# Sorting the edges of a graph layer: turned keys and weights copied bank by bank, the last seven swaps moved behind the sort, the first 128 columns ahead of the rest

## The chip, the cores and the metric

The kernel runs on one core of one Trainium2 chip. The metric is the device time of one execution in microseconds (us). Three runs of the kernel before gave 2411.13, 2404.05 and 2411.05 us, with the median 2411.05. A further execution was profiled: it took 2398.86 us, and its trace spans 2397.1 us. Engines are named as the profile names them: PE (matmuls), PEld (its weight loads), DVE (vector), ACT (scalar), POOL (GpSimd) and SP (which issues transfers).

## What is computed

The reference is a layer on a graph with 6250 nodes, 256 features and 100,000 edges, followed by a mixture of 16 experts. Only its first part matters here:

```python
feats = jnp.einsum('nf,hfo->hno', xn, W)                  # 4 heads of 64
z = s_self[:, edge_row] + s_neigh[:, edge_col]
e = jnp.where(z > 0, z, 0.2 * z) * edge_weight
alpha = segment_softmax(e, edge_row)                      # per row of the graph
out = segment_sum(alpha[:, None] * feats[edge_col], edge_row)
x = x + relu(out + bias) + mix(xn)                        # mix: linear attention
x = x + ffn(layernorm(x))                                 # top 2 of 16 experts
```

The edges come in no order of `src` that the kernel may rely on. It sorts them by `src` itself, with the destination in the low bits of each key and the edge's weight carried along. It can then sum the edges of a node tile with matmuls.

## The kernel before

**Stage one** is `nodes_and_sort`. It normalises 49 tiles of 128 nodes, projects them (PE, with POOL and ACT beside it) and stores the features to HBM (`feat_d`) for the gathers of stage two. In the same block DVE runs a bitonic sort of 128 x 784 (padded to 896) keys. Keys and weights lie in `big`, each in two buffers of 128 x 896 (`key`, `wgt`), and the steps go from one buffer to the other.

- A **swap** compares columns at a distance of 2^bit. DVE writes the mask, the minima and the maxima (L507 to L509; L511 to L513 where the columns don't pair evenly). ACT copies the old weights into the other buffer (L296), and DVE then exchanges the weights whose mask is set with a predicated copy (L522; L527 and L528). A predicated copy waits for the mask and for ACT's copy; ACT's next copy waits for the predicated copy.
- A **turn** transposes the 128 x 896 array, since swaps reach over columns only. PE transposes seven blocks of 128 columns into two PSUM banks of 512 columns, first the keys (into `p_turn`, then a semaphore `k_turned`), then the weights (into `p_kv`, then `w_turned`). DVE copies the keys back (L448, with a piece of 16 x 128 at L450 for turns back). ACT copies the weights back (L306, L308), and after that does its copy for the next swap (L296). There are 20 turns.
- A **sign** step flips the sign of some keys in place (L478).

A planner with costs (3.0 for a swap, 4.0 for a turn) puts 108 of the 190 steps beside the node tiles, where PE is busy. The other 82 are `rest`, run alone, with nine turns among them. The last of `rest` are a turn and the seven swaps of bits 6 to 0. Then the stage ends, and all engines meet at a barrier.

**Stage two** is `edge_stream`. The sorted edges are 784 used chunks of 128 edges each (one partition of one block of 128 columns is a chunk). Wherever a chunk crosses into another node tile it is taken once for each, which gives 832 places of (chunk, tile) pairs, in 26 blocks of 32. A preparation on DVE, PE and ACT builds for each pair its chunk number, its destinations (`pair_idx`), weights (`pair_w`) and places in the tile: masks of 128 x 416 (L1208), a matmul that counts them, one-hot picks (L1225), matmuls that select columns (L1154), and copies out of PSUM on ACT (L985, L989). In the trace the PSUM tiles are all named `wide`.

Then, for each pair, POOL issues an indirect DMA that gathers 128 rows of `feat_d` into a ring of 64 places in `big` (L934). It begins when ACT has copied the first half of `pair_idx` (`pool.wait_ge(pair_copied, 1)`). From the 65th on it waits until PE has summed the pair that held the place 64 before. DVE needs the 32 gathers of block k before it makes the scores of block k (L1301); it does this ten pairs into the summing of block k-1. From the scores come, over DVE, PE and ACT, the softmax numerators. Then for each pair ACT scales the rows (L961), PE sums them (L1057), and DVE adds the sum to the node tile (L1367). The first 13 blocks also carry the key-value products of the linear attention.

After stage two come routing, experts and the output. They read nothing else from the sort.

Of the kernel before, what the change touches and what calls it, by code (L numbers as in the profile page):

```python
# [61 lines left out]
def nodes_and_sort(nc, ctx, a, m):  # L62
# [31 lines left out]
    def inside(lo, *dims):  # L94
# [55 lines left out]
        sem("k_turned"), sem("w_turned"), sem("k_back"), sem("w_back"), sem("signed"))  # L150
    half_signed, masked, part_made, parity_made = sem("half_signed"), sem("masked"), sem("part_made"), sem("parity_made")
# [21 lines left out]
    m["sorted_in"] = buf  # L173

# [38 lines left out]
    with nc.Block() as block:  # L213
# [72 lines left out]

        def copy_weights(act, entry):

            kind, k, arg, buf, late, without, n = entry
            if kind == "swap":  # L290
                cols = slice(0, live(k, arg >= 7))
                if n["swap"]:
                    act.wait_ge(w_swapped, n["swap"])
                if n["turn"]:
                    act.wait_ge(w_back, n["turn"])
                nc.scalar.activation(wgt[:, 1 - buf, cols], wgt[:, buf, cols], ACT.Copy).then_inc(w_copied, 1)  # L296

        def weights_back(act, entry, via):
# [4 lines left out]
            to = wgt[:, 1 - buf, :]  # L303
            act.wait_ge(w_turned, n["turn"] + 1)
            width = live(k, True) if arg else WHOLE
            ins = nc.scalar.activation(to[:, 0:width], via[:, 0:width], ACT.Copy)  # L306
            if not arg and not without:
                ins = nc.scalar.activation(to[0:LATE, WHOLE:WIDE], via[0:LATE, WHOLE:WIDE], ACT.Copy)  # L308
            ins.then_inc(w_back, 1)

        @block.scalar
        def _(act):
# [57 lines left out]
            for entry in rest:  # L370
                copy_weights(act, entry)
                weights_back(act, entry, p_kv[1])

        @block.vector
        def _(dve):
# [67 lines left out]
            def keys_back(entry):  # L443
                kind, k, turned, buf, late, without, n = entry
                to = key[:, 1 - buf, :]
                dve.wait_ge(k_turned, n["turn"] + 1)
                width = live(k, True) if turned else WHOLE
                ins = nc.vector.tensor_copy(to[:, 0:width], p_turn[:, 0:width])  # L448
# [38 lines left out]
            def swap(entry):  # L487
# [32 lines left out]
                dve.wait_ge(masked, n["swap"] + 1)  # L520
                if whole:
# [34 lines left out]
        def _(pe):  # L556
# [24 lines left out]
            def keys_over(entry):  # L581
# [66 lines left out]
def edge_stream(nc, ctx, a, m):  # L648
# [116 lines left out]
    last = big[0:1, 4 * CH:4 * CH + PAIRS]  # L765
# [1591 lines left out]
```

## Time and profile before

| what | before |
|---|---|
| runs, median (lowest to highest) | 2411.05 us (2404.05 to 2411.13) |
| profiled execution, its span | 2398.86 us, 2397.1 us |
| node tiles end, sort runs alone from about | 333 us |
| last swap of the sort ends | 531 us |
| first gather starts | 546.37 us |
| last gather starts | 1613.89 us |
| stage two ends about | 1667 us |
| experts and output | 1800 to 2397 us |

Over the whole span PE is busy 70% of the time, DVE 73%, ACT 58% and POOL 55%. These are means over very different stages, and the table says where each begins. A row of the timeline gives start, duration, engine, line, operation, out<-in with shapes, and in brackets how long the engine had been idle before and what released it.

### The profile page before, as it was taken

To read this page: it belongs to the slowest core of one execution; us is meant where nothing else is said; L and a number is where in the kernel's file an instruction comes from. 1 tells how busy PE (TensorE), PEld (TensorE's weight loads), DVE (VectorE), ACT (ScalarE), POOL (GpSimd) and SP (SyncE) were. 2 spreads that over 40 slices of the span, in tenths; PEclk is the share of its full clock that TensorE was granted. 3 is DMA by queue.
4 is the path that set the end of the run, shared out by engine and by line. 5 is a ranking of instruction groups with operands and counts; after the bars stand their busy time and mean duration, and the time that the engine had idled before them with its cause. 6 is when DMAs were issued, how large, how long until landed. Compare 5 with 4: busy or idle time off the path is not lost. (4 is left out here: it accounts for less than half of the span.)

```text
span 2397.1 us, 38652 instructions
## 1 busy us (share of the span) xinstructions
PE 1681.5 (70%) x8046; PEld 1259.4 (53%) x8046; DVE 1756.0 (73%) x4645; ACT 1393.3 (58%) x4627; POOL 1309.4 (55%) x1245
## 2 busy tenths in 40 slices
PE   3899961115676777777767888766641999999965
PEld 2455531012454555555445555533541999999854
DVE  6988899985588888899867777677860555555468
ACT  2555553322687887879786878796430444444344
POOL 2333310006777777777777777770575555555521
PEclk9999985557678777767888989888555999999988
DMA  6333320005456565564746555541970333333354
GB/s 206 132 124 138 135 88 0 0 29 173 141 153 203 165 201 165 165 196 138 221 136 180 151 159 154 163 115 37 259 102 18 104 106 106 103 105 106 95 176 153
DMA packets 167253, 317.72 MB, mean 133 GB/s; under 512 B 34358, under 2 KB 102627, under 8 KB 167089
## 3 DMA queue, kind: packets, MB, share of 16 engines
q1 hardware_dynamic: 104654, 166.68, 20.9%
q0 software_dynamic: 54176, 140.57, 20.7%
q10 hardware_dynamic: 8256, 8.68, 2.0%
q8 instruction: 55, 0.90, 0.2%
q14 instruction: 112, 0.89, 0.1%
HBM read 248.17 MB, written 67.65 MB: 132 GB/s over the span
## 5 line engine op out<-in xcount | busy, mean ns | idle before, releaser
L934 POOL DMA_INDIRECT big<-feat_d,pair_idx x832 | 815.3, 980 | 265.7 <-issue 188.9
L961 ACT ACTIVATE big<-big 128x64 f32<-128x64 f32 x3328 | 800.5, 333 | 0.9
L1057 PE MATMUL wide<-big 128*128 128x260 f32 x1664 | 606.5, 488 | 152.8 <-DVE big L1367 113.7
L1057 PEld LDWEIGHTS wide<-big 128*128 128x128 f32 x1664 | 332.8, 231 | 249.9 <-issue 210.6
L1367 DVE TENSOR_TENSOR big<-big,wide 128x260 f32 x832 | 350.9, 422 | 119.1 <-PE wide L1057 52.5
L1348 DVE TENSOR_TENSOR big<-wide,pair_rel 128x128 f32<-128x128 f32 x832 | 233.6, 282 | 0.0
L296 ACT ACTIVATE big<-big 128x896 f32<-128x896 f32 (+2 forms) x153 | 136.9, 895 | 161.4 <-DVE big L522 147.6
L2051 PEld LDWEIGHTS p_h<-xT,w_sb 128*128 128x128 f32 x1808 | 220.4, 193 | 5.7
L2051 PE MATMUL p_h<-xT,w_sb 128*128 128x128 f32 x1808 | 220.8, 276 | 0.0
L268 POOL TENSOR_SCALAR xn<-X,mean,rstd 128x256 f32<-128x256 f32 x49 | 101.8, 2078 | 210.4 <-PE p_t L600 177.8
L2062 PE MATMUL p_o<-w_sb,hT 128*128 128x256 f32 x904 | 213.9, 379 | 1.1 <-DVE w_sb L2000 1.1
L2000 DVE COPY w_sb<-big 128x1024 f32 x113 | 84.1, 744 | 169.9 <-PE p_o L2062 169.9
L1941 POOL DMA_INDIRECT moe_d<-x_out,x_to x113 | 115.5, 1022 | 151.1 <-DVE x_idx L1980 111.2
L1955 ACT ACTIVATE xT<-p_x 128x256 f32<-128x256 f32 x113 | 43.4, 384 | 256.1 <-PE p_x L2040 256.1
L522 DVE COPY_PREDICATED big<-big 128x896 f32<-128x896 uint32 (+2 forms) x150 | 163.9, 1093 | 23.2 <-ACT big L296 22.8
L625 PE MATMUL p_kv<-big,xnT_s 128*128 128x512 f32 x392 | 177.2, 595 | 0.0
L2062 PEld LDWEIGHTS p_o<-w_sb,hT 128*128 128x128 f32 x904 | 162.9, 190 | 19.0 <-DVE w_sb L2000 1.5
L1964 ACT ACTIVATE hT<-p_h,b1T 128x128 f32<-128x128 f32 x452 | 128.9, 368 | 58.5 <-issue 54.4
L1933 POOL DMA_INDIRECT xs<-y_d,x_idx x113 | 130.4, 1154 | 46.3 <-issue 34.2
L1024 PEld LDWEIGHTS wide<-score_parts,hot_t 128*128 128x128 bf16 x832 | 91.0, 109 | 99.1 <-issue 47.6
L1633 POOL DMA_INDIRECT list_d<-pair_i,place_i x98 | 103.0, 1052 | 53.5 <-issue 29.6
L573 PE MATMUL p_turn<-ident,big 128*128 128x128 f32 x120 | 22.3, 337 | 156.0 <-DVE big L509 152.7
(329 smaller groups left out, 2675.9 us busy)
## 6 DMA issues: line engine op xcount, KB each, us to landing
big<-code_d SPq DMA_DIRECT2D x52, 512.0 KB
kv_d<-big SPq DMA_DIRECT2D x49, 512.0 KB, 2.6
X<-kv_d SPq DMA_DIRECT2D x12, 2048.0 KB, 13.0
big<-in_L_ffn_w_dram SPq DMA_DIRECT2D x32, 512.0 KB
b_sb<-in_L_ffn_b_dram SPq DMA_DIRECT2D x113, 128.0 KB, 3.0
big<-feat_d,pair_idx POOLq DMA_INDIRECT x832
big<-moe_d SPq DMA_DIRECT2D x7, 1792.0 KB, 9.9
feat_d<-feat_sb SPq DMA_DIRECT2D x49, 130.0 KB, 2.7
```

The lines of the kernel that those rows point to most:

```text
L296: nc.scalar.activation(wgt[:, 1 - buf, cols], wgt[:, buf, cols], ACT.Copy).then_inc(w_copied, 1)
L522: ins = nc.vector.copy_predicated(paired(w2[:, 0:whole], bit), mk.bitcast(U32).unsqueeze(2).to_broadcast([P, whole >> (bit + 1), 2, 1 << b ...
L625: last = nc.tensor.matmul(p_kv[par][:, n * INNER:(n + 1) * INNER], xnT_s[:, par, b, :], wqkv[:, b, (n + 1) * INNER:(n + 2) * INNER], start ...
L934: nc.gpsimd.indirect_dma_start(out=rows[:, n // SB % RB, n % SB, :], out_offset=None, in_=m["feat_d"], in_offset=bass.IndirectOffsetOnAxis ...
L961: ins = nc.scalar.activation(rows[:, b, s, cols], rows[:, b, s, cols], ACT.Copy, scale=rows[:, b, s, HF + h:HF + h + 1])
L1057: nc.tensor.matmul(sums[s % RING][:, 0:HF + H], onehot[:, s // GP % 2, s % GP, :], rows[:, b, s, :], start=True, stop=True).then_inc(summe ...
L1348: nc.vector.tensor_tensor(onehot[:, at // GP, at % GP, :], lane_p, pair_rel[:, ds(k * SB + s, 1)].to_broadcast([P, P]), ALU.is_equal).then ...
L1367: nc.vector.tensor_tensor(of, of, sums[s % RING][:, 0:HF + H], ALU.add).then_inc(added, 1)
L1933: nc.gpsimd.indirect_dma_start(out=xs[:, w, :], out_offset=None, in_=m["y_d"], in_offset=bass.IndirectOffsetOnAxis(idx[:, w:w + 1].bitcast ...
L1964: last = nc.scalar.activation(hT[:, par, f, :], p_h[par][:, f * P:(f + 1) * P], ACT.Relu, bias=b1T[:, ds(e * FB + f, 1)])
L2051: last = nc.tensor.matmul(p_h[par][:, cols], w1[:, par, b * F + f * P:b * F + (f + 1) * P], xT[:, par, b, :], start=(b == 0), stop=(b == K ...
L2062: last = nc.tensor.matmul(p_o[par][:, 0:D], hT[:, par, f, :], w2[:, at:at + D], start=(f == 0), stop=(f == FB - 1))
```

## The change

Three things are edited.

1. **Turns.** PE signals after the first four transposes (the first bank) as well as after all seven. DVE copies the keys of the first bank, 128 x 512, and then the other 256 or 272 columns. ACT copies the weights in the same two pieces.
2. **Weights behind the nodes.** For the turns of `rest` but the first, the weights aren't copied back into `wgt` first. The first swap after such a turn takes them from the PSUM bank: ACT makes its one copy from `p_kv`, and DVE's predicated copy reads `p_kv`.
3. **The last seven swaps** leave `nodes_and_sort`, which now ends with the turn. `edge_stream` begins with them, split in two. First all seven for the keys of columns 0 to 127, then from their first 128 chunks the first 64 entries of `pair_idx`, with the seven weight swaps of these columns around it. Then follow the seven swaps of the other 768 columns. POOL waits for the first 64 entries alone (`f_copied`) and for the old semaphore only at the 65th gather.

```diff
+    plan, final = plan[:-7], plan[-7:]
+    m["final"] = [(j, at) for _, _, j, at, *_ in final]
...
+    looped = plan[at][-1]["turn"]
+    straight = {n["swap"]: arg >= 7 for kind, k, arg, buf, late, without, n in rest
+                if kind == "swap" and n["turn"] > looped and arg in (6, k - 1)}
...
+        def turned_weights(act, to, via, turns, width, tail, done):
+            width = WHOLE if tail else width
+            act.wait_ge(w_first, turns)
+            nc.scalar.activation(to[:, 0:512], via[:, 0:512], ACT.Copy)
+            act.wait_ge(w_turned, turns)
+            ins = nc.scalar.activation(to[:, 512:width], via[:, 512:width], ACT.Copy)
+            if tail:
+                ins = nc.scalar.activation(to[0:LATE, WHOLE:WIDE], via[0:LATE, WHOLE:WIDE], ACT.Copy)
+            ins.then_inc(done, 1)
...
             if kind == "swap":
-                cols = slice(0, live(k, arg >= 7))
+                width = live(k, arg >= 7)
+                if n["swap"] in straight:
+                    turned_weights(act, wgt[:, 1 - buf, :], p_kv[1], n["turn"], min(width, LIVE), width == WIDE, w_copied)
+                    return
...
             for entry in rest:
                 copy_weights(act, entry)
-                weights_back(act, entry, p_kv[1])
+            assert rest[-1][0] == "turn"
+            weights_back(act, rest[-1], p_kv[1])
...
+                width = live(k, True) if turned else WHOLE
+                dve.wait_ge(k_first, n["turn"] + 1)
+                nc.vector.tensor_copy(to[:, 0:512], p_turn[:, 0:512])
                 dve.wait_ge(k_turned, n["turn"] + 1)
-                ins = nc.vector.tensor_copy(to[:, 0:width], p_turn[:, 0:width])
+                ins = nc.vector.tensor_copy(to[:, 512:width], p_turn[:, 512:width])
...
+                if n["swap"] in straight:
+                    w1 = p_kv[1]
...
-                flip(entry, key, p_turn, 0, range(7)).then_inc(k_turned, 1)
+                flip(entry, key, p_turn, 0, range(4)).then_inc(k_first, 1)
+                flip(entry, key, p_turn, 0, range(4, 7)).then_inc(k_turned, 1)
...
-                    pe.wait_ge(w_back, n["turn"])
-                flip(entry, wgt, via, 0, range(7)).then_inc(w_turned, 1)
+                    pe.wait_ge(w_back, min(n["turn"], looped))
+                flip(entry, wgt, via, 0, range(4)).then_inc(w_first, 1)
+                flip(entry, wgt, via, 0, range(4, 7)).then_inc(w_turned, 1)
...
-            pool.wait_ge(pair_copied, 1)
+            pool.wait_ge(f_copied, 1)
             for n in range(PAIRS):
+                if n == F:
+                    pool.wait_ge(pair_copied, 1)
...
+            for n in range(4):
+                copy_lead(n)
+            act.wait_ge(f_idx, 1)
+            nc.scalar.activation(pair_idx[:, 0:F], first_idx, ACT.Copy).then_inc(f_copied, 1)
+            for n in range(4, 7):
+                copy_lead(n)
+            for n, (_, at) in enumerate(m["final"]):
+                if n:
+                    act.wait_ge(rest_weights, n)
+                nc.scalar.activation(m["wgt"][:, 1 - at, P:CH], m["wgt"][:, at, P:CH], ACT.Copy).then_inc(rest_copied, 1)
...
+            pe.wait_ge(f_passes, 1)
+            nc.tensor.matmul(first_chunk, ones_b, first_passes, start=True, stop=True).then_inc(f_chunk, 1)
+            pe.wait_ge(f_code, 1)
+            pe.wait_ge(f_pick, 1)
+            nc.tensor.matmul(first_idx, first_dst, first_pick, start=True, stop=True).then_inc(f_idx, 1)
...
+            def swap_keys(bit, at, cols, mk, masked, swapped):
+                lo, hi = halves(m["key"][:, at, cols], bit)
+                to = halves(m["key"][:, 1 - at, cols], bit)
+                nc.vector.tensor_tensor(folded(mk, bit), lo, hi, ALU.is_gt).then_inc(masked, 1)
+                nc.vector.tensor_tensor(to[0], lo, hi, ALU.min)
+                nc.vector.tensor_tensor(to[1], lo, hi, ALU.max).then_inc(swapped, 1)
...
+            for n, (bit, at) in enumerate(m["final"]):
+                if n:
+                    dve.wait_ge(lead_keys, n)
+                swap_keys(bit, at, LEAD, lead_mask(n), lead_masked, lead_keys)
+            dve.wait_ge(lead_keys, 7)
             nc.vector.memset(first_row[:, HF:HF + H], TINY).then_inc(first_made, 1)
             dve.wait_ge(first_in, 16)
...
+            nc.vector.tensor_scalar(first_passes, iota_f[:, 0:F], step_f[:, 0:1], None, ALU.is_gt).then_inc(f_passes, 1)
...
+            nc.vector.tensor_scalar(first_dst, first_code[:, 0:P], N - 1, None, ALU.min).then_inc(f_code, 1)
+            for n in range(3):
+                lead_swap(n)
+            dve.wait_ge(f_chunk, 1)
+            nc.vector.tensor_scalar(first_pick, first_chunk, place_f[:, 0:1], None, ALU.is_equal).then_inc(f_pick, 1)
+            for n in range(3, 7):
+                lead_swap(n)
+            for n in range(7):
+                rest_swap(n)
```

`lead_swap(n)` is the predicated copy of step n over columns 0 to 127 (it waits for ACT's copy n and for the lead swap before it), and `rest_swap(n)` is a whole swap over the other 768.

The order in which the instructions stand shows the move. DVE at the end of the sort, before (`X` holds the bias row there, `ahead` begins the preparation):

```order
L507 TENSOR_TENSOR big<-big 128x448
L508 TENSOR_TENSOR big<-big 128x448
L509 TENSOR_TENSOR big<-big 128x448
L522 COPY_PREDICATED big<-big 128x896
L213 UNCONDITIONAL_BRANCH
L1189 UNCONDITIONAL_BRANCH
L1195 MEMSET X 128x4
L1197 TENSOR_SCALAR X<-X 128x256
L1199 TENSOR_SCALAR ahead<-place_f 128x7
```

The same place now, where the two branches are the barrier:

```order
L466 COPY big<-p_turn 128x256
L468 COPY big<-p_turn 16x128
L220 UNCONDITIONAL_BRANCH
L1246 UNCONDITIONAL_BRANCH
L1262 TENSOR_TENSOR big<-big 128x64
L1263 TENSOR_TENSOR big<-big 128x64
L1264 TENSOR_TENSOR big<-big 128x64
```

and, after the seven lead swaps of the keys, the first pairs' chain and the rest:

```order
L1313 TENSOR_SCALAR big<-big,step_f 128x64
L1314 TENSOR_SCALAR big<-big 128x128
L1315 TENSOR_SCALAR big<-big 128x128
L1269 COPY_PREDICATED big<-big 128x128 x3
L1319 TENSOR_SCALAR big<-wide,place_f 128x64
L1269 COPY_PREDICATED big<-big 128x128 x4
L1262 TENSOR_TENSOR big<-big 128x384
L1263 TENSOR_TENSOR big<-big 128x6x64
L1264 TENSOR_TENSOR big<-big 128x6x64
L1269 COPY_PREDICATED big<-big 128x768
```

So the barrier has moved ahead of the seven swaps, and `ahead` and all that follows it stand behind them. ACT at the last two turns, before:

```order
L306 ACTIVATE big<-p_kv 128x784
L296 ACTIVATE big<-big 128x784 x10
L306 ACTIVATE big<-p_kv 128x768
L308 ACTIVATE big<-p_kv 16x128
L296 ACTIVATE big<-big 128x896 x7
L213 UNCONDITIONAL_BRANCH
L938 UNCONDITIONAL_BRANCH
L985 ACTIVATE hot_t<-wide 128x416
```

and now:

```order
L298 ACTIVATE big<-p_kv 128x512
L300 ACTIVATE big<-p_kv 128x272
L317 ACTIVATE big<-big 128x784 x9
L298 ACTIVATE big<-p_kv 128x512
L300 ACTIVATE big<-p_kv 128x256
L302 ACTIVATE big<-p_kv 16x128
L220 UNCONDITIONAL_BRANCH
L972 UNCONDITIONAL_BRANCH
L1022 ACTIVATE big<-big 128x128 x4
L1027 ACTIVATE pair_idx<-wide 128x64
L1022 ACTIVATE big<-big 128x128 x3
L1033 ACTIVATE big<-big 128x768 x7
```

The ten copies of `wgt` after a turn have become nine, since the first one now comes from PSUM, and the small copy of `pair_idx` stands ahead of the seven copies of the rest. On POOL only the wait in front of the 832 gathers differs.

## Rows read from the trace of the kernel before

**Rows 1.** Page, costliest groups: count, busy us, mean ns, idle before, releaser.

```profile
L934 POOL DMA_INDIRECT big<-feat_d,pair_idx x832 | 815.3, 980 | 265.7 <-issue 188.9
```

**Rows 2.** Timeline of POOL: the first, the 32nd and the last of 832 gathers.

```profile
546.37 1.52 POOL L934 DMA_INDIRECT big<-feat_d,pair_idx  x1 [12.59 <-ACT pair_idx L989]
...
588.15 0.94 POOL L934 DMA_INDIRECT big<-feat_d,pair_idx  x1 [0.30 <-issue]
...
1613.89 0.95 POOL L934 DMA_INDIRECT big<-feat_d,pair_idx  x1 [0.30 <-issue]
```

**Rows 3.** Gathers in one stretch: length, busy us (count), PEclk, DMA share, GB/s.

```profile
717.00:1173.00 456.00, 348.79 (x353) 0.75 0.57 175
```

**Rows 4.** Timeline of DVE, line L1301: the scores of single blocks.

```profile
590.96 0.37 DVE L1301 TENSOR_TENSOR z<-wide,big 128x128 f32<-128x128 f32 x1 [13.07 <-DMA big<-feat_d,pair_idx]
631.54 0.38 DVE L1301 TENSOR_TENSOR z<-wide,big 128x128 f32<-128x128 f32 x1 [11.92 <-DMA big<-feat_d,pair_idx]
674.15 0.38 DVE L1301 TENSOR_TENSOR z<-wide,big 128x128 f32<-128x128 f32 x1 [1.79 <-DMA big<-feat_d,pair_idx]
717.71 0.38 DVE L1301 TENSOR_TENSOR z<-wide,big 128x128 f32<-128x128 f32 x1 [2.30 <-DMA big<-feat_d,pair_idx]
...
1133.36 0.37 DVE L1301 TENSOR_TENSOR z<-wide,big 128x128 f32<-128x128 f32 x1
1172.92 0.38 DVE L1301 TENSOR_TENSOR z<-wide,big 128x128 f32<-128x128 f32 x1 [3.10 <-DMA big<-feat_d,pair_idx]
```

**Rows 5.** Timeline of PE and DVE: one turn back, in `rest`.

```profile
371.53 1.54 PE L573 MATMUL p_turn<-ident,big 128*128 128x128 f32 x6 [16.68 <-DVE big L509]
...
373.18 0.96 DVE L448 COPY big<-p_turn 128x768 f32<-128x768 f32 x1 [0.77 <-PE p_turn L573]
...
376.17 1.01 DVE L522 COPY_PREDICATED big<-big 128x768 f32<-128x768 uint32 x1 [0.43 <-ACT big L296]
```

**Rows 6.** Waits of DVE from 336 to 511 us: total us, times, longest.

```profile
DVE big L448 <- PE p_turn L573: 3.1, 4, 0.8
DVE big L448 <- PE p_turn L578: 1.9, 2, 1.0
DVE big L448 <- PE p_turn L575: 1.8, 2, 1.0
DVE big L522 <- ACT big L296: 1.5, 4, 0.5
DVE big L527 <- ACT big L296: 0.9, 2, 0.5
```

**Rows 7.** Timeline of ACT and DVE: from the last turn to the scores.

```profile
511.85 0.25 ACT L308 ACTIVATE big<-p_kv 16x128 f32<-16x128 f32 x1
...
532.40 0.06 DVE L1195 MEMSET X<- 128x4 f32 x1 [1.32 <-PEq L2305]
...
535.55 0.16 DVE L1199 TENSOR_SCALAR ahead<-place_f 128x7 f32<-128x7 f32 x1
...
577.55 0.34 DVE L1295 TENSOR_SCALAR from_last<-far_rel 128x128 f32<-128x128 f32 x1
```

**Rows 8.** Timeline of DVE: sizes of single instructions in the sort.

```profile
378.63 1.00 DVE L522 COPY_PREDICATED big<-big 128x768 f32<-128x768 uint32 x1
...
436.21 0.42 DVE L512 TENSOR_TENSOR big<-big 128x256 f32<-128x256 f32 x1
...
436.97 0.17 DVE L512 TENSOR_TENSOR big<-big 128x16 f32<-128x16 f32 x1
```

**Rows 9.** Timeline of POOL and DVE: gathers beside DVE's work on SBUF.

```profile
558.42 1.61 POOL L934 DMA_INDIRECT big<-feat_d,pair_idx  x1 [0.30 <-issue]
...
560.18 1.01 DVE L1254 TENSOR_TENSOR big<-big 1x832 f32<-1x832 f32 x1
...
576.64 1.20 POOL L934 DMA_INDIRECT big<-feat_d,pair_idx  x1 [0.30 <-issue]
```

**Rows 10.** Tile `xn`: POOL's normalising beside the sort, ns min/median/max.

```profile
L268 POOL TENSOR_SCALAR xn<-X,mean,rstd x49: 1208/2061/3125, 37.3 to 315.7; 128x256 f32<-128x256 f32 x49
```

More of the change, by code:

```diff
@@ L173, in nodes_and_sort @@
     m["sorted_in"] = buf
+    plan, final = plan[:-7], plan[-7:]
+    assert all(kind == "swap" for kind, *_ in final)
+    m["final"] = [(j, at) for _, _, j, at, *_ in final]
     GROUPS = NT // GT
@@ L294, in copy_weights @@
                 if n["turn"]:
-                    act.wait_ge(w_back, n["turn"])
-                nc.scalar.activation(wgt[:, 1 - buf, cols], wgt[:, buf, cols], ACT.Copy).then_inc(w_copied, 1)
+                    act.wait_ge(w_back, min(n["turn"], looped))
+                nc.scalar.activation(wgt[:, 1 - buf, 0:width], wgt[:, buf, 0:width], ACT.Copy).then_inc(w_copied, 1)
         def weights_back(act, entry, via):
@@ L302, in weights_back @@
                 return
[L303 to L309, printed above, removed]
+            turned_weights(act, wgt[:, 1 - buf, :], via, n["turn"] + 1, live(k, True), not arg and not without, w_back)
         @block.scalar
@@ L765, in edge_stream @@
     last = big[0:1, 4 * CH:4 * CH + PAIRS]
+    F = RB * SB
+    fresh = line[:, CH + PAIRS:]
+    first_dst, first_pick, first_passes = fresh[:, 0:P], fresh[:, P:P + F], fresh[:, P + F:P + F + F // 2].bitcast(BF16)
+    first_chunk, first_idx = wide[2][:, 0:F], wide[2][:, 512:512 + F]
+    first_code = spare_k.bitcast(I32)
+    mask = big[:, 6 * CH + 1024:6 * CH + 1024 + 448]
     place_f, step_f, step_i = sb("place_f", [P, Q]), sb("step_f", [P, Q]), sb("step_i", [P, Q], I32)
@@ L982, in step, with copy_lead @@
                     exponents(k + 1, 1 - b)
+            def copy_lead(n):
+                _, at = m["final"][n]
+                if n:
+                    act.wait_ge(lead_weights, n)
+                nc.scalar.activation(m["wgt"][:, 1 - at, 0:P], m["wgt"][:, at, 0:P], ACT.Copy).then_inc(lead_copied, 1)
+            for n in range(4):
[8 more added lines that the diff above has]
+                nc.scalar.activation(m["wgt"][:, 1 - at, P:CH], m["wgt"][:, at, P:CH], ACT.Copy).then_inc(rest_copied, 1)
             act.wait_ge(chunk_done, 1)
@@ L989, in take @@
                 nc.scalar.activation(out, bank, ACT.Copy).then_inc(pair_copied, 1)
-            take(1, pair_idx[:, 0:half], wide[1][:, 0:half])
+            take(1, pair_idx[:, F:half], wide[1][:, F:half])
             take(3, pair_w[:, 0:half], wide[3][:, 0:half])
@@ new lines, in swap_weights @@
+            def swap_weights(bit, at, cols, mk, swapped):
+                width = cols.stop - cols.start
+                pairs = "p (g two c) -> p g two c"
+                nc.vector.copy_predicated(
+                    m["wgt"][:, 1 - at, cols].rearrange(pairs, two=2, c=1 << bit),
+                    folded(mk, bit).bitcast(U32).unsqueeze(2).to_broadcast([P, width >> (bit + 1), 2, 1 << bit]),
+                    m["wgt"][:, at, cols].rearrange(pairs, two=2, c=1 << bit)[:, :, ::-1, :]).then_inc(swapped, 1)
@@ new lines, in _, with lead_mask, lead_swap, rest_swap @@
+            LEAD, REST = slice(0, P), slice(P, CH)
+            def lead_mask(n):
+                return mask[:, n * P // 2:(n + 1) * P // 2]
+            def lead_swap(n):
+                bit, at = m["final"][n]
+                dve.wait_ge(lead_copied, n + 1)
+                dve.wait_ge(lead_masked, n + 1)
+                if n:
+                    dve.wait_ge(lead_weights, n)
+                swap_weights(bit, at, LEAD, lead_mask(n), lead_weights)
+            def rest_swap(n):
+                bit, at = m["final"][n]
+                if n:
+                    dve.wait_ge(rest_keys, n)
+                    dve.wait_ge(rest_weights, n)
+                else:
+                    dve.wait_ge(lead_weights, 7)
+                swap_keys(bit, at, REST, mask[:, 0:(CH - P) // 2], rest_masked, rest_keys)
+                dve.wait_ge(rest_copied, n + 1)
+                dve.wait_ge(rest_masked, n + 1)
+                swap_weights(bit, at, REST, mask[:, 0:(CH - P) // 2], rest_weights)
```

19 lines of the change are left out of this document (18 added, 1 removed).

## The prediction

> **What bounds the kernel now.** I read the page's costliest groups first, then the timeline of the engine that leads them, then its waits, and last the stretch in which it has not begun.
>
> The costliest group is POOL's 832 gathers [rows 1]. They start at 546.37 and the last starts at 1613.89 [rows 2], so 1067.5 us, or 1.28 us each, is nearly half the time. All idle time in front of one is 0.30 us; it is never longer, whatever releaser the row names, so POOL issues without a real wait from first to last. In the blocks that carry the attention products the rate is 456/353 = 1.29 us [rows 3]. If nothing stops POOL, the end of stage two moves one for one with its first gather.
>
> The consumers (DVE, ACT, PE) could forbid that. The scores of a block show who waits [rows 4]. Those of blocks 0 to 3 wait 13.07, 11.92, 1.79 and 2.30 us for gathers. From block 4 to 13 they wait hardly at all. With block 14 the wait is back, 3.10. So in the middle the consumers go at (1133.36 - 717.71)/10 = 41.6 us a block, and POOL at 32 x 1.29 = 41.3. They are level there, and an earlier POOL is worth something only if the consumers are earlier too by block 3.
>
> Ahead of 546.37 nothing runs beside the sort from about 333 on: DVE is the path, with short waits at each turn [rows 5, 6].
>
> **The change part by part.**
>
> *Turns, keys.* In `rest` PE's six whole transposes take 1.54 us, and DVE then copies for 0.96 after an idle 0.77 [rows 5]. The first four end two transposes before the sixth, 0.51 us at most (1.54/6 each); since they overlap I take 0.45. DVE can begin that much earlier. The first copy (512 columns, about 0.65 by the rate of 0.96 for 768) covers the last transposes, and the split costs one more start, some 0.05. I take 0.40 a turn. Eight turns wait on PE, with 3.1 + 1.9 + 1.8 = 6.8 us in all [rows 6], so the gain is 3.2 us; the ninth turn, the first of `rest`, is met by DVE still busy and gives nothing. Ends: 0, if the second copy waits as long as the whole did; 6, if nearly all idle goes.
>
> *Turns, weights.* The predicated copy waits 1.5 + 0.9 = 2.4 us for ACT [rows 6], because ACT copies twice in a row after a turn. One copy is gone and the other begins earlier, so all 2.4 go. Next late is the mask, DVE's own. The predicated copy now reads PSUM; no row shows that. The key copy from PSUM (0.96 for 768) and the predicated copy from SBUF (1.00 for 768, [rows 8]) have one column rate, so I charge 0.05 each, 0.4 in eight, and keep 0 to 1.6. **Turns together: 5.2 us, between 2 and 8.** The eleven turns beside the node tiles get an instruction more on DVE and on ACT. I cost that at nothing, covered by PE's matmuls on the tiles; without that cover it is 11 x 0.1 us.
>
> *The sort's end to the first gather, without the turns' gain.* Before, keys and weights of the last turn are back at 511.85 + 0.25 = 512.1 [rows 7]. With the split ACT ends about 0.4 earlier, 511.7. The barrier takes 1.3 (the 1.32 ahead of 532.40 in rows 7), so the new block begins at 513.0. What then stands ahead of the first gather:
> - seven lead swaps of keys, three instructions on 64 columns. 0.42 us for 256 and 0.17 for 16 [rows 8] give 0.22 for 64. They overlap by 0.08 within a swap and not between swaps, 0.52 a swap: 3.65. The bias row's transfer, over within 3 us of the block's start (532.40 to 535.55 in rows 7), is covered by it.
> - the bias row, three instructions of one column, the mask, the two for the destinations: about 1.5 (0.16 us and a wait each for the small ones, as at 535.55 in rows 7).
> - three lead weight swaps, each a predicated copy (0.30 for 128 columns, by 1.00 for 768) and ACT's copy (0.25 for 128 columns in rows 7) in turn, with two hops 0.65: 1.9.
> - the pick (0.2), a matmul on 64 columns and its hops (0.5, an estimate from two transposes), ACT's copy (0.2), and 0.3 on POOL, as ahead of every gather: 1.2.
>
> The sum is 8.2, so the first gather starts at 521.2 instead of 546.37: **25.2 us earlier, and 30.4 with the turns.** Nothing queued behind POOL's wait is hurt, since the gathers are all it has. The second wait, at gather 65, is met: those entries were copied before the first gather at the old pace, about as late as 551 now, and gather 65 comes near 600.
>
> *What the early gathers run into.* They now run beside DVE's swaps of 768 columns, 7 x 2.46 us (376.17 to 378.63 in rows 5 and 8) = 17.2, and beside the first 10 us of the preparation. A gather takes 0.95 alone, but 1.61 beside tensor-tensor instructions on SBUF and 1.20 beside a fast tensor-scalar one [rows 9]. POOL's normalising, beside the very same swaps, takes 2.06 for its 1.21 at best [rows 10], 0.85 more. I take 0.75 more in the swaps: 17.2/2.0 = 8.6 gathers where 13.8 would be issued, 5.2 x 1.25 = 6.5 us lost. In the 10 us I take 0.25 more: 1.7 us. **Loss 8.2 us.** Ends: 0, and 12.7 (a gather that waits out two instructions, 2.75 each in the swaps, and 0.6 more in the preparation). **POOL: 30.4 - 8.2 = 22.2 us earlier.** The bounds together give 15 to 33.
>
> *The consumers.* DVE's preparation from 535.55 to 577.9 [rows 7] is 42.3 us and stays. It now begins after the lead work (3.65 + 1.7 + seven lead weight swaps at 0.65 = 9.9) and the 17.2: 513.0 - 5.2 + 27.1 = 534.9. It ends at 577.2, 13.8 us ahead of the 590.96 at which block 0's scores ran. The waits of blocks 1 to 3 (16.0 us) can go too, so the consumers can be 29.8 us earlier by block 3. That is more than POOL's 22, so POOL sets the end.
>
> **Sum.** 2398.86 - 22.2 = 2376.7 for a run like the profiled one. That run was 12 us below the median, and the gain is in no part that differs between runs, so from 2411.05 I forecast **2389 us**.
>
> **Rivals.**
>
> *DVE is held up by the gathers (slower).* Some 45 gathers now lie beside DVE's chain from 516 to 577. If each stalls it by its whole slot of 1.25, the chain ends 56 us later. Then the consumers are late through block 13 (1133.36 - 29.8 + 56 = 1159.6). POOL can be only ten gathers ahead of what they need there, and restarts from the 458th. Before, that one was issued about 1141.7: block 14's last, the 480th, landed at 1172.92 [rows 4], less 22 x 1.29, less 2.8 for landing (the 32nd, issued at 588.15 in rows 2, landed at 590.96). So it is 18 us slower, 2429. It turns at a stall of 38 us; below 31 the kernel is over 0.3% faster, above 45 over 0.3% slower. (0.3%, 7 us, is about what a measurement can tell from no change.) Against it: the tensor-tensor instruction at 560.18 took 1.01 between gathers [rows 9], and 1.02 is what 832 columns take by the rates of rows 8.
>
> *An exclusive lock (no change).* As a mechanism of this kernel: a gather that starts first holds DVE off for its 0.95 us. 45 x 0.95 = 43 us of stall, 5 us slower, 2416. Its chance is 0.05. The same row speaks against it. The Trainium skill has this as a rule ("SBUF — State Buffer", section "SBUF: two separate sides"): the pair of ports that the two engines share goes to whichever starts first for its whole instruction, and the other fully blocks. By that rule the time would be this rival's; the trace shows POOL blocked and DVE not.
>
> *The first pairs come later than summed.* The chain has some 30 hops between instructions and engines. If each costs the 0.3 us that stands ahead of a gather on POOL, and not the few hundredths I gave it, it is 8 us longer. The gain is then 14, or less if the gathers starve further as well: 7 to 14, 2400.
>
> *The ports cost nothing.* Then POOL would be 30.4 earlier and the consumers (29.8) about level: 2381, inside the range.
>
> **How the numbers follow.** The forecast with its bounds (15 to 33 us, the free ports included): 0.73. Late first pairs: 0.11. Stall near the turning point (the lock's 0.05 and any other of 31 to 45 us), no change: 0.09. Slower: 0.07. So faster by over 0.3% is 0.84, within 0.09, slower 0.07. The range: 2411.05 - 33 = 2378, less half of the 12 us by which runs differ, 2372; at the other end 2411.05 - 15 = 2396 and half of the late case, 2404. That leaves out under 0.2.
>
> **What would show it.** The first gather near 516; gathers of 1.6 to 2.0 us until about 535 and of 0.95 from about 560; block 0's scores near 577, with no wait for gathers there and short ones at blocks 2 and 3; the last gather near 1592. Waits of the predicated copies on ACT are gone at the turns, and DVE's idle time at a turn is about 0.3. It would be wrong if the instructions of 384 columns in the new block took more than their 0.56, if the scores of block 0 came after 590, or if POOL's idle time showed waits on PE's sums.

## The result and the profile after

The changed kernel took 2374.36 us, median of four runs (2372.4 to 2375.83); four runs of the kernel before, beside it, had the median 2410.07. The medians differ by 35.7 us. The ratio is 0.9865, with the 95% interval 0.9837 to 0.9892, which is 32.5 us, with 26 to 39 inside the interval. The forecast was 2389, with the range 2372 to 2404. Both kernels were compared twice more, each time on one chip: 2371.28 against 2400.33 (ratio 0.9882, 0.9862 to 0.9903) and 2373.63 against 2404.76 (0.9876, 0.986 to 0.9893). So the gain is 29 to 36 us by the medians and 28 to 33 by the ratios, and the forecast of 22.2 was low. The times below leave out one slow execution, of 5376.25 us, among the ten of `stall_30`.

One sentence of the part on the change has to be put right. The weights go straight from the bank after every turn of `rest` but the last, the first one included. The last turn's weights are copied back, since its swaps follow in the next block.

The profiled execution of the changed kernel took 2375.39 us, with a span of 2373.6. The page's costliest group, which answers [rows 1]:

```profile
L968 POOL DMA_INDIRECT big<-feat_d,pair_idx x832 | 821.4, 987 | 260.0 <-issue 189.2
```

The timeline of POOL shows the first, the 32nd, the 65th and the last gather:

```profile
515.35 1.29 POOL L968 DMA_INDIRECT big<-feat_d,pair_idx  x1 [6.86 <-ACT pair_idx L1027]
...
561.39 1.68 POOL L968 DMA_INDIRECT big<-feat_d,pair_idx  x1 [0.30 <-issue]
...
604.61 0.95 POOL L968 DMA_INDIRECT big<-feat_d,pair_idx  x1 [0.30 <-issue]
...
1589.03 0.95 POOL L968 DMA_INDIRECT big<-feat_d,pair_idx  x1 [0.30 <-issue]
```

The 65th gather of the kernel before, which [rows 2] leave out:

```profile
630.00 0.94 POOL L934 DMA_INDIRECT big<-feat_d,pair_idx  x1 [0.30 <-issue]
```

The first gather starts 31.0 us earlier and the last one 24.9 earlier. POOL has the same 0.30 us in front of each gather as before, with no wait from first to last. What it lost on the way it lost inside the gathers: the 64 slots up to the 65th take 89.3 us (515.35 to 604.61), and before the change they took 83.6 (546.37 to 630.00).

DVE's waits from 336 to 506 us show the turns. One line is left of the five of [rows 6]:

```profile
DVE big L464 <- PE p_turn L593: 2.6, 8, 0.3
```

The timeline of DVE, ACT and POOL shows the chain from the last turn to the first gather:

```profile
504.37 0.27 DVE L468 COPY big<-p_turn 16x128 f32<-16x128 f32 x1
...
507.09 0.23 DVE L1262 TENSOR_TENSOR big<-big 128x64 f32<-128x64 f32 x1 [2.45 <-PEq L2433]
...
511.02 0.15 DVE L1310 TENSOR_SCALAR step_i<-big 128x1 int32<-128x1 int32 x1
...
513.50 0.30 DVE L1269 COPY_PREDICATED big<-big 128x128 f32<-128x128 uint32 x1 [0.38 <-ACT big L1022]
513.71 0.28 DVE L1319 TENSOR_SCALAR big<-wide,place_f 128x64 f32<-128x64 f32 x1
...
514.83 0.22 ACT L1027 ACTIVATE pair_idx<-wide 128x64 int32<-128x64 f32 x1 [0.69 <-PE wide L1199]
```

Seven lead swaps of keys and the bias row take the time from 507.09 to 511.02. The first pick (L1319) stands behind three lead weight swaps, of which the second and the third each wait 0.38 for ACT. From the block's start to the first gather it is 8.26 us.

The scores of blocks 0 to 3, 13 and 14 (DVE, line L1429) answer [rows 4]:

```profile
578.79 0.36 DVE L1429 TENSOR_TENSOR z<-wide,big 128x128 f32<-128x128 f32 x1
607.28 0.37 DVE L1429 TENSOR_TENSOR z<-wide,big 128x128 f32<-128x128 f32 x1
648.85 0.39 DVE L1429 TENSOR_TENSOR z<-wide,big 128x128 f32<-128x128 f32 x1 [0.58 <-DMA big<-feat_d,pair_idx]
691.89 0.38 DVE L1429 TENSOR_TENSOR z<-wide,big 128x128 f32<-128x128 f32 x1 [1.74 <-DMA big<-feat_d,pair_idx]
...
1107.18 0.38 DVE L1429 TENSOR_TENSOR z<-wide,big 128x128 f32<-128x128 f32 x1 [0.51 <-DMA big<-feat_d,pair_idx]
1147.55 0.37 DVE L1429 TENSOR_TENSOR z<-wide,big 128x128 f32<-128x128 f32 x1 [3.62 <-DMA big<-feat_d,pair_idx]
```

The waits of 13.07 and 11.92 us in blocks 0 and 1 are gone. From block 3 on the consumers are 25 to 26 us earlier, as POOL is.

### The profile page after: what moved, and what is told of

It reads as the page before. It is cut to its first block and busy times, and to the rows that moved or that the text cites. A ratio compares the mean times of both kernels' runs of the same rounds, so it can differ in the third digit from the quotient of the medians.

```text
span 2373.6 us, 38726 instructions
## 1 busy us (share of the span) xinstructions
PE 1689.5 (71%) x8049; PEld 1267.0 (53%) x8049; DVE 1757.1 (74%) x4700; ACT 1389.7 (59%) x4647; POOL 1331.8 (56%) x1245
## 5 line engine op out<-in xcount | busy, mean ns | idle before, releaser
L317 ACT ACTIVATE big<-big 128x896 f32<-128x896 f32 (+2 forms) x138 | 123.4, 895 | 153.8 <-DVE big L542 140.2
L2128 DVE COPY w_sb<-big 128x1024 f32 x113 | 78.6, 695 | 174.9 <-PE p_o L2190 174.9
L2069 POOL DMA_INDIRECT moe_d<-x_out,x_to x113 | 130.7, 1157 | 136.2 <-DVE x_idx L2108 95.5
L542 DVE COPY_PREDICATED big<-big 128x896 f32<-128x896 uint32 (+2 forms) x137 | 149.5, 1091 | 22.9 <-ACT big L317 22.7
L2061 POOL DMA_INDIRECT xs<-y_d,x_idx x113 | 131.1, 1160 | 45.9 <-issue 33.5
L1761 POOL DMA_INDIRECT list_d<-pair_i,place_i x98 | 103.2, 1053 | 53.5 <-issue 29.6
```

Source lines behind the costliest of these rows:

```text
L542: ins = nc.vector.copy_predicated(paired(w2[:, 0:whole], bit), mk.bitcast(U32).unsqueeze(2).to_broadcast([P, whole >> (bit + 1), 2, 1 << b ...
L2061: nc.gpsimd.indirect_dma_start(out=xs[:, w, :], out_offset=None, in_=m["y_d"], in_offset=bass.IndirectOffsetOnAxis(idx[:, w:w + 1].bitcast ...
L2069: nc.gpsimd.indirect_dma_start(out=m["moe_d"], out_offset=bass.IndirectOffsetOnAxis(to[:, w:w + 1].bitcast(U32), 0), in_=out[:, w % 2, :], ...
```

## The experiments

**The parts alone.** `turns_only` is the kernel before with the edits of the turns. `early_only` is the changed kernel with the turns as before. Of `early_only`, the core of the diff against the changed kernel (the weights are undone in the same way):

```diff
-                dve.wait_ge(k_first, n["turn"] + 1)
-                nc.vector.tensor_copy(to[:, 0:512], p_turn[:, 0:512])
                 dve.wait_ge(k_turned, n["turn"] + 1)
-                ins = nc.vector.tensor_copy(to[:, 512:width], p_turn[:, 512:width])
+                ins = nc.vector.tensor_copy(to[:, 0:width], p_turn[:, 0:width])
```

> The kernel before with the edits of the turns alone (copies bank by bank, weights straight from the bank), the seven last swaps still in the sort. My theory: the sort ends 6 us earlier (DVE's 7.0 us of waits at turns gone, less a second start per turn), every later event moves with it, gain 6 us. Rival (the barrier or the bias row's transfer takes it back, or the turns' gain is lost beside the node tiles): gain under 2 us.

> The changed kernel with the turns as in the kernel before: only the move of the last seven swaps and the early first 64 gathers. My theory: first gather 6 us later than in the changed kernel (near 521.5), end 6 us later, gain 17 to 18 us against a profiled run of 2399, 29 against a median of 2410. Rival (the consumers set the end, and the turns matter more through block 0's scores than through POOL): gain of under 12 against the profiled run.

Measured beside one kernel before (2406.42): `turns_only` 2399.24, ratio 0.9976 (0.9961 to 0.999), so 5.8 us less by the ratio; `early_only` 2379.99, ratio 0.9901 (0.9882 to 0.9919), so 23.8 us less. By its ratios the whole change gave 28.3 and 29.8 on the other chips, and 32.5 in the first comparison. The sum of the parts is 29.6, so they add up within their intervals (2.4 to 9.4 and 19.7 to 28.4), and the early end is four fifths.

**Keys without weights.** `early_keys` keeps the split of the key copies, and copies the weights back in one piece:

```diff
-    straight = {n["swap"]: arg >= 7 for kind, k, arg, buf, late, without, n in rest
-                if kind == "swap" and n["turn"] > looped and arg in (6, k - 1)}
+    straight = {}
...
-            act.wait_ge(w_first, turns)
-            nc.scalar.activation(to[:, 0:512], via[:, 0:512], ACT.Copy)
             act.wait_ge(w_turned, turns)
-            ins = nc.scalar.activation(to[:, 512:width], via[:, 512:width], ACT.Copy)
+            ins = nc.scalar.activation(to[:, 0:width], via[:, 0:width], ACT.Copy)
```

> The changed kernel with part of the turn edits undone: keys are still copied bank by bank, but the turned weights go back into their buffer in one copy after all seven transposes, for every turn, and the swap after it takes them from there. Theory (keys and weights of a turn each bring what the waits of the kernel before say): the waits of the predicated copies on ACT behind the turns are back, some 2.4 us in all up to the block's start, the waits of the key copies on PE stay gone (about 3.5 us); the first gather 2.4 to 3 us later than in the changed kernel, and so gather 65 and the end. Rival (the key copies alone bring the 6 us that the turn edits brought when they were made alone): first gather within 0.5 us of the changed kernel's.

Both the theory and its rival missed. The first gather came at 522.69, 6.4 us later than the 516.26 of the changed kernel on the same chip (2378.28 against 2373.63 in time). The waits of DVE in `early_keys` from 336 to 512 us, in total, times and longest:

```profile
DVE big L538 <- ACT big L314: 3.3, 5, 1.1
DVE big L460 <- PE p_turn L589: 2.5, 8, 0.3
DVE big L543 <- ACT big L314: 2.0, 2, 1.1
```

The waits on PE are down from 6.8 to 2.5, but those on ACT are up from 2.4 to 5.3. One turn shows how. DVE in the kernel before, then in `early_keys`:

```profile
481.99 0.97 DVE L448 COPY big<-p_turn 128x784 f32<-128x784 f32 x1 [0.83 <-PE p_turn L575]
...
485.41 0.46 DVE L527 COPY_PREDICATED big<-big 128x272 f32<-128x272 uint32 x1 [0.54 <-ACT big L296]
```

```profile
482.63 0.69 DVE L460 COPY big<-p_turn 128x512 f32<-128x512 f32 x1 [0.20 <-PE p_turn L589]
...
486.69 0.46 DVE L543 COPY_PREDICATED big<-big 128x272 f32<-128x272 uint32 x1 [1.12 <-ACT big L314]
```

The key copy waits 0.63 less, and the predicated copy 0.58 more. From the first key copy of `rest` to the end of the last one it is 176.4 us before (334.45 to 510.86), 176.2 in `early_only`, 175.9 in `early_keys`, and 169.7 in the changed kernel. So splitting the keys alone is worth 0.3 to 0.5 us, and together with the weights 6.7. The two paths meet at the predicated copy, and the weights' was the longer one. The weights without the keys were not run.

**The same kernels again.** `b_again`, `b_third` are the kernel before and `after_again`, `after_third` the changed one, unedited. They were to tell how much of 35.7 is steady.

> The kernel before, once more, with its own trace. Question: why the timed gain (36 us) is 12 us larger than the gain between the two profiled runs (23.5 us). Theory A (the runs of the kernel before vary, 2399 to 2411 us, in the blocks 4 to 13 of stage two, where consumers and POOL are level, and those of the changed kernel vary less): times spread over some 5 to 12 us, and a trace of a run near 2410 shows blocks 4 to 13 longer by about 10 us than the 415.7 us of the first trace. Theory B (the first profiled run was one odd execution): the new profiled run is near 2410 and its times spread by under 4 us, with the difference in another stage.

> The changed kernel once more, unedited, beside the others: 2374 by the first runs. If its gain of 35.7 us rather than 23.5 (the two profiled runs) is steady, 2370 to 2378 against 2404 to 2411; if the first comparison was drawn from the edges of two spreads, a gain of 24 to 30 us. Trace: first gather near 515.4, block 0's scores near 579, last gather 1586 to 1592; the gathers' own busy time, which differed by 1% between runs, says which part of the spread is theirs.

> The kernel before, unedited, for a third trace of it on the chip on which the changed kernel is traced too. Two traces had the first gather at 546.37 and 549.04 us, though the sort ended within 0.3 us of each other. If the bias row's transfer and the late clock of TensorE cost 2 to 3 us in most executions, the first gather is near 549, gather 65 near 632.5 and the last gather near 1616.5; if the later trace was the exception, near 546.4, 630 and 1614.

> The changed kernel, unedited, beside the kernel before on one chip. Of the parts measured apart (turn edits 5.8 us, the first columns' early end 23.8 us) the sum is 29.6 us; the gain should be 27 to 32 us, with the first gather near 516, gather 65 near 604.5 and the last gather 1585 to 1589, and no wait of POOL over 0.31 us from the first gather to the last.

Starts of three gathers, in us, from the traces of POOL:

| run | first | 65th | last | profiled time |
|---|---|---|---|---|
| before, `b_again`, `b_third` | 546.37, 549.04, 549.99 | 630.00, 632.73, 633.54 | 1613.89, 1616.64, 1617.23 | 2398.86, 2402.46, 2405.99 |
| after, `after_again`, `after_third` | 515.35, 516.42, 516.26 | 604.61, 604.30, 604.49 | 1589.03, 1585.43, 1585.14 | 2375.39, 2370.68, 2373.02 |
| mean gain | 32.5 | 27.6 | 29.4 | 29.4 |

The kernel before spreads by 5.6 us over the twelve runs of `b_again` (2401.02 to 2406.64), but its blocks 4 to 13 took 417.1 us there (719.91 to 1137.05), only 1.5 more than in the first trace. So theory B is out, and theory A has the spread but not its place (the traced run, at 2402.46, wasn't near 2410). `after_again` gave 29.1 us, the second of its two cases. `b_third` had the first gather at the place that was named for it, but only in part for the reason that was named: its block began 2.0 us later, its bias row was awaited 2.77 us, and from `ahead` to the first gather it took 1.7 longer than the first trace, at a granted clock of 0.67 (546 to 550 us). `after_third` came out in every line.

The profiled run on which the sum was made was the earliest of three: its 65th gather is 2.1 us ahead of the mean. Part of this is in the preparation. The timelines of DVE and POOL in `b_again` show it, where the sort ended 0.3 earlier than in the first trace and the first gather came 2.7 later:

```profile
532.10 0.06 DVE L1195 MEMSET X<- 128x4 f32 x1 [1.32 <-PEq L2305]
536.38 0.29 DVE L1197 TENSOR_SCALAR X<-X 128x256 f32<-128x256 f32 x1 [4.22 <-DMA X<-in_L_gnn_bias_dram]
...
549.04 1.47 POOL L934 DMA_INDIRECT big<-feat_d,pair_idx  x1 [15.57 <-ACT pair_idx L989]
```

The bias row was awaited 4.22 us, and 2.87 in the first trace. The granted clock differs in the matmuls that select `pair_idx`. Windows of the kernel before in its first trace and in `b_again` (columns as in [rows 3], for each engine, PEclk behind POOL's):

```profile
544.00:548.00 4.00, 4.00 (x13) 2.24 (x12) 3.86 (x10) 0.52 (x1) 1.52 (x1) 1.00 0.53 208
```

```profile
545.00:549.00 4.00, 4.00 (x8) 2.03 (x7) 3.86 (x10) 0.52 (x1) 0.00 (x0) 0.60 0.20 74
```

PE did thirteen matmuls in four microseconds at 2.4 GHz, and eight at a mean of 0.60, so mostly at 1.2 GHz. From `ahead` to the first gather it is 10.82 us in the first trace and 12.45 in `b_again`. In both PE had stood for 2.07 us just ahead of these matmuls, waiting for DVE. In the changed kernel the lead swaps cover most of the transfer (0.39 us were left of the wait in `after_again`, none in the other two traces), and only three small matmuls stand ahead of the first gather. It came within 1.1 us in three traces (515.35 to 516.42), and within 3.6 before, 2.0 of which were there when the block began.

**POOL held back.** `hold_first` keeps all of the change but the early start:

```diff
             pool.wait_ge(f_copied, 1)
+            pool.wait_ge(pair_copied, 1)
```

> The changed kernel, but POOL waits for the old half of pair_idx before its first gather, as before; everything else stays, the split swaps too. My theory (POOL's first gather sets the end): first gather near 547.3, end about 1 us after that of the kernel before (2400 to 2411, as its runs). Rival (the gain came from consumers that are ready earlier, not from the early gathers): the gain stays above 10 us.

It took 2405.1, ratio 0.9997 (0.9984 to 1.001): the whole gain is gone. That of the turns is gone too, since the lead work now stands ahead of the preparation (`ahead` begins at 536.52 here, and at 535.55 to 537.47 in three traces of before). The first gather starts at 549.35. So POOL's first gather is what sets the end. It also shows what the gathers do to DVE. DVE from 513 to 560, grouped by line and shape (count, busy us, mean ns, idle before); the changed kernel with gathers beside it from 515 on:

```profile
L1269 DVE COPY_PREDICATED big<-big 128x768 f32<-128x768 uint32 x7 | 7.0, 1005 | 0.0
L1262 DVE TENSOR_TENSOR big<-big 128x384 f32<-128x384 f32 x7 | 3.9, 560 | 0.7
L1264 DVE TENSOR_TENSOR big<-big 128x384 f32<-128x384 f32 x7 | 3.9, 551 | 0.0
```

and `hold_first`, with none until 549:

```profile
L1270 DVE COPY_PREDICATED big<-big 128x768 f32<-128x768 uint32 x7 | 7.0, 1005 | 0.0
L1263 DVE TENSOR_TENSOR big<-big 128x384 f32<-128x384 f32 x7 | 3.9, 558 | 0.7
L1265 DVE TENSOR_TENSOR big<-big 128x384 f32<-128x384 f32 x7 | 3.9, 551 | 0.0
```

The means are equal to 2 ns. Of these two engines POOL pays alone; its timeline in the changed kernel, beside the swaps:

```profile
521.19 1.52 POOL L968 DMA_INDIRECT big<-feat_d,pair_idx  x1 [0.30 <-issue]
523.01 1.33 POOL L968 DMA_INDIRECT big<-feat_d,pair_idx  x1 [0.30 <-issue]
524.65 1.28 POOL L968 DMA_INDIRECT big<-feat_d,pair_idx  x1 [0.30 <-issue]
```

These three repeat with each two swaps: 1.68 us a gather, where 1.25 is the slot alone.

**DVE held up by hand.** `stall_12` and `stall_30` are the changed kernel with 20 and 52 chained memsets of PSUM on DVE ahead of the swaps of 768 columns:

```diff
+            for n in range(52):
+                chain(nc.vector.memset(wide[3][:, 0:512], 0.0))
             for n in range(7):
                 rest_swap(n)
```

> The same with 20 memsets, about 12 us. Theory: the 13.8 us that block 0's scores have in hand take this: first gather near 515, block 0's scores near 591, waits for gathers in blocks 0 to 3 gone, and an end within 3 us of the changed kernel's. Rival (the consumers' chain moves the end one for one): 12 us more than the changed kernel. Rival (POOL's start alone): no change either; the run with 30 us tells that one apart.

> The changed kernel with 52 memsets of 128 x 512 in a chain on DVE between the lead weight swaps and the swaps of the other 768 columns: about 30 us of DVE time (to be read from the trace), in which POOL gathers on; it stands in for DVE being held up. Theory (POOL's first gather sets the end unless the consumers are so late that POOL, which can be 64 gathers ahead, has to wait for places of the ring): first gather near 515; block 0's scores near 579 + 30 = 609; the consumers go level with POOL up to block 13, so block 13's scores would come near 1107 + 30 - 4 = 1133 (4 us of waits for gathers in blocks 1 to 3 are used up first), and POOL, waiting for places, restarts some 16 us later than in the changed kernel: 16 us more than the changed kernel, some 8 to 12 us less than before. Rival (the consumers' chain moves the end one for one): 30 us more than the changed kernel, slower than before. Rival (POOL's start alone counts): no change against the changed kernel.

The times were 2378.87 and 2399.05, against 2371.28 for the changed kernel beside them: 7.6 and 27.8 us more. Both are more than the theory gave, and less than the stall itself. The stalls were longer than planned, as the group of the memsets in `stall_30` shows (busy, mean ns, idle before):

```profile
L1323 DVE MEMSET wide<- 128x512 f32 x52 | 25.2, 485 | 9.4 <-DVE wide L1323 9.3
```

That is 34.6 us. Against `after_again`, block 0's scores came 13.0 and 37.1 us later (592.84 and 616.98 against 579.86). The rest is in one place, the 64th and 65th gather of POOL's timeline, in `stall_12` and then in `stall_30`:

```profile
602.07 0.95 POOL L968 DMA_INDIRECT big<-feat_d,pair_idx  x1 [0.30 <-issue]
612.13 0.94 POOL L968 DMA_INDIRECT big<-feat_d,pair_idx  x1 [9.11 <-PE wide L1108]
```

```profile
605.03 1.02 POOL L968 DMA_INDIRECT big<-feat_d,pair_idx  x1 [0.30 <-issue]
636.21 0.94 POOL L968 DMA_INDIRECT big<-feat_d,pair_idx  x1 [30.15 <-PE wide L1108]
```

POOL runs 64 gathers into the ring and then waits for the first sum, once. The wait ends 19.3 and 19.2 us after block 0's scores (592.84 to 612.13, 616.98 to 636.21). From there the 767 other gathers take 981.4 and 983.3 us, as ever. So the 65th gather stands at POOL's own time or 19.3 us behind block 0's scores, whichever is later: 7.8 and 31.9 us later than in `after_again` (604.30), and the time follows, not to the microsecond (7.6 and 27.8 by the medians, 8.5 and 35.1 between the profiled executions). The theory's mechanism held and its place was wrong: it let the ring fill up at block 14. Both rivals fall, one for one with `stall_12` (7.6 of 13.0), POOL's start alone with both.

For the changed kernel this gives what the consumers have in hand. Its 65th gather could go at 579.86 + 19.3 = 599.2 and goes at 604.30: 5.1 us, and 6.5 in the first trace. The gathers that ran beside the memsets are of use too, from the timeline of `stall_30`:

```profile
521.08 0.95 POOL L968 DMA_INDIRECT big<-feat_d,pair_idx  x1 [0.30 <-issue]
522.34 0.95 POOL L968 DMA_INDIRECT big<-feat_d,pair_idx  x1 [0.30 <-issue]
```

So these memsets cost a gather nothing. They write PSUM, and they also read nothing; four instructions of the changed kernel's preparation tell the two apart:

```profile
545.36 1.01 DVE L1360 TENSOR_TENSOR big<-big,hot_t 128x832 f32<-128x832 f32 x1
545.52 1.67 POOL L968 DMA_INDIRECT big<-feat_d,pair_idx  x1 [0.30 <-issue]
...
552.82 0.94 POOL L968 DMA_INDIRECT big<-feat_d,pair_idx  x1 [0.30 <-issue]
552.96 1.02 DVE L1369 SCALAR_TENSOR_TENSOR big<-big,wide 128x832 f32<-128x832 f32 x1 [3.60 <-PE wide L1210]
...
556.68 1.49 DVE L1376 MEMSET pen_run<- 1x1716 bf16 x1 [0.31 <-issue]
556.98 0.94 POOL L968 DMA_INDIRECT big<-feat_d,pair_idx  x1 [0.30 <-issue]
...
558.20 1.01 DVE L1379 COPY big<-wide 1x832 f32<-1x832 f32 x1
558.22 0.94 POOL L968 DMA_INDIRECT big<-feat_d,pair_idx  x1 [0.30 <-issue]
```

All four write SBUF (`big`, `pen_run`). The gather took 1.67 beside the one with both inputs in SBUF, and 0.94 beside those that have an input in PSUM (`wide`) or none. So writing SBUF isn't what costs a gather here; the dear rows, these and those of the swaps, are ones in which DVE reads all its inputs from SBUF, though not every such gather was slow (the second one, at 516.95, took 0.95 beside the first swap). ACT's copies aren't the cause either: in the kernel before ACT copied within SBUF from 564.43 to 575.80, and the gathers at 566.45, 567.70 and 568.95 took 0.95.

**The pick ahead of the weights.** `pick_sooner` lets the first pick pass the lead weight swaps, and moves the bias row behind them:

```diff
-            for n in range(3):
-                lead_swap(n)
             dve.wait_ge(f_chunk, 1)
             nc.vector.tensor_scalar(first_pick, first_chunk, place_f[:, 0:1], None, ALU.is_equal).then_inc(f_pick, 1)
-            for n in range(3, 7):
+            for n in range(7):
                 lead_swap(n)
...
```

Not shown are the bias row's lines, and the change on ACT: two copies of lead weights, and not four, now stand ahead of the copy of `pair_idx`.

> The changed kernel with two moves on DVE: the bias row's two instructions stand behind the lead weight swaps, and the first pick, with no lead weight swap ahead of it, directly behind the matmul that counts; ACT copies two old lead weights ahead of its copy of the first indices, and not four. Theory (the first gather sets the end one for one): first gather 1.5 to 2 us earlier, near 513.6, and 1.5 us off the end, which is too little to be told in the time, but shows in the trace. Rival (the first pick waits on PE's count anyway, so DVE only idles): first gather within 0.4 us of 515.35 and no gain.

The timeline of `pick_sooner`:

```profile
512.63 0.28 DVE L1314 TENSOR_SCALAR big<-wide,place_f 128x64 f32<-128x64 f32 x1
...
513.76 0.22 ACT L1027 ACTIVATE pair_idx<-wide 128x64 int32<-128x64 f32 x1 [0.29 <-PE wide L1199]
...
514.28 1.29 POOL L968 DMA_INDIRECT big<-feat_d,pair_idx  x1 [5.18 <-ACT pair_idx L1027]
```

The first gather comes 2.1 us earlier than in `after_again`, the 65th 1.7 and the last 3.0 (1582.42). The time, 2371.01 against 2371.28, doesn't tell the two apart. More of this kind would end at the 5 us that the consumers have in hand, by the estimate above.

## Why the prediction was right, and where it was off

*What bounds the kernel.* Right, by `hold_first`: all else in place, the first gather at its old time gives the old time.

*Turns.* 6.7 us where 5.2 was forecast. The sum's parts weren't as told. The keys' 3.2 and the weights' 2.4 were added as if each could be had alone; `early_keys` has the keys without the weights and gains 0.3 to 0.5. The sum survived because both edits were made. The waits themselves fell by 4.2 (PE) and 2.4 (ACT), 6.6 together: DVE began a turn's keys 0.53 earlier (4.2 over eight turns), where I took 0.45. The 0.4 for PSUM was too much: from 336 to 506 us, five predicated copies of 768 columns from `p_kv` took a mean of 999 ns, and 39 from `wgt` 1007. The eleven turns beside the node tiles cost nothing that shows: `rest` starts at 334.89 to 335.90 in three traces after, and at 334.20 to 336.48 before.

*The chain to the first gather.* 8.2 forecast, 8.26 measured. Its parts: 3.9 with the start of the bias row where 3.65 and a share of 1.5 stood, the lead weight swaps at 0.68 each where 0.65 stood. The rival of late first pairs falls, and the cover of the bias row held.

*Loss of the gathers beside DVE.* This was the mis-sized step. I took 2.0 us a gather beside the swaps, from POOL's normalising beside the same swaps [rows 10], and 8.2 us in all. The gathers went at 1.68. The first 64 slots took 89.3, 87.9 and 88.2 us, against 83.5 to 83.7 before, which is 4.8 us more on average. By what the single gathers took over 0.95, the swaps cost 4.0 us where I took 6.5, and the 10 us behind them 0.5 to 0.7 where I took 1.7. As a stand-in for a gather the normalising was too dear; why a gather loses less beside the same swaps no run shows.

*The consumers.* Right: `ahead` at 534.65 (534.9 forecast), block 0's scores at 578.79 (577), no wait for gathers there. The lead of the consumers over POOL (29.8 against 22.2) came out as the 5.1 to 6.5 us in hand.

*Sum.* The forecast gain of 22.2 and the 29.4 of the last gather (mean of three traces each) differ by 7.2, but for rounding: 3.4 from the loss (8.2 less 4.8), 2.1 from the trace that served as the base (the first gather at 546.37, mean 548.47), and 1.8 from the 767 later gathers (983.8 before, 982.1 after). The sentence that the gain is in no part that differs between runs was wrong: the bias row's transfer and TensorE's clock did differ there, and the change hides most of both. The rest, from 29.4 to 35.7, is put down to the spread of four runs against four, as the two later comparisons gave 29.1 and 31.1.

*The rivals.* The stall of DVE didn't come: `hold_first` and the changed kernel have equal durations. Its price was worked out at the wrong place: I let the ring stop POOL at the 458th gather, and in `stall_30` it stopped POOL at the 65th, and no later gather waited over 0.36. By the 65th gather the turning point against the first trace is 630.0 - 19.3 - 577.2 = 33.5 us of stall, and I said 38. `stall_30`, with its 37 us, was level with the kernel before (ratio 0.9991, 0.9981 to 1.0001), which doesn't tell the two apart. The exclusive lock falls by the same rows. By the Trainium skill ("SBUF — State Buffer", section "SBUF: two separate sides") a GpSimd operation that reads SBUF and starts first would hold the ports that it shares with DVE for its whole instruction, and fully block a DVE operation with two SBUF inputs. Here POOL was delayed (0.95 to as much as 1.53) and DVE's swaps by no more than 2 ns.

**What stays open.** The 767 gathers behind the 65th take 983.7 to 983.9 us in three traces of the kernel before, 980.7 to 984.4 in the changed one, but 974.9 in `early_only`, 976.0 in `early_keys` and 988.0 in `turns_only`. Most of it is made in the gathers up to about the 450th, by their own durations. What in a program decides it wasn't found. It is up to 13 us, more than the gain of the turns, and it is why the times of these three don't follow their first gathers to the microsecond.

## What to carry to other kernels

When one engine issues at a steady rate to the end, a microsecond off the start of its first instruction is worth as much as one off its work. Build the few inputs that it needs to begin ahead of the rest, and check with a stall made by hand how late the consumers may be. Look for that limit where the ring is full for the first time, not where the next stage begins. When two paths meet at one instruction, the waits on both are one term, and shortening only the one that isn't last gives nearly nothing (0.3 to 0.5 us of 6.7 here).

## What was not expected of the hardware

A gather on POOL beside DVE's swaps on SBUF took 0.95 to 1.53 us and DVE's instructions no longer (560 against 558 ns); beside memsets into PSUM or SBUF, and beside instructions with an input in PSUM, it took 0.94 to 0.95, as alone. The transfer of one bias row was awaited 2.77, 2.87 and 4.22 us in three executions of one program, and the same matmuls ran in a window at a granted clock of 1.00 in one and 0.60 in another.
